# A third kept score tile in a two-sweep latent attention, with the shift additions on GpSimd

## The chip, the cores and the metric

The kernel runs on one core of one Trainium2 chip. A core has TensorE (PE, matrix products; PEld is its weight loading), VectorE (DVE), ScalarE (ACT), GpSimd (POOL) and SyncE (SP, which only issues DMAs here), and the memories SBUF and PSUM. The engines run on their own and wait for one another on semaphores. The metric is the device time of one execution in microseconds (us), as the median of several runs.

## The reference

The program is a chain of six layers on `x` (512 rows of 512) with a context `ctx_1024` of 8192 rows: a blockwise MLP over the context, a Mamba-like scan, a quantised feed-forward layer, the latent cross attention which the change touches, a channel attention, and a mixture of experts. The fourth one is:

```python
def _L1_xattn_ref(x, latents, Wq, Wkv, Wout, gm, bm, gl, bl):   # x: the context, latents: the normed rows
    scale = D_HEAD ** (-0.5)
    xn = layernorm(x, gm, bm)
    ln = layernorm(latents, gl, bl)
    q = ln @ Wq
    kv_input = jnp.concatenate([xn, ln], axis=-2)
    kv = kv_input @ Wkv
    k, v = jnp.split(kv, 2, axis=-1)
    q, k, v = (heads(q), heads(k), heads(v))
    q = q / scale
    sim = jnp.einsum('bhid,bhjd->bhij', q, k)
    sim = sim - jax.lax.stop_gradient(jnp.max(sim, axis=-1, keepdims=True))
    attn = jax.nn.softmax(sim, axis=-1)
    out = jnp.einsum('bhij,bhjd->bhid', attn, v)
    return out.transpose(0, 2, 1, 3).reshape(B, L, H * dh) @ Wout
```

There are 8 heads of 64, 512 queries and 8704 keys (8192 of the context and the 512 latents).

## The kernel before

The attention works in two sweeps over 17 chunks of 512 keys (`KCHUNKS`, `KEYS`). Heads are taken in four pairs (`PAIRS`), two heads side by side on the two halves of the partitions. All products are made in three parts out of a high and a low half of each float32 operand.

**First sweep** (`project_pe`, `project_act`, `project_dve`, 835 to 1320 us). PE projects the keys and values of chunk c, ACT evicts them, POOL makes the low halves of the context rows (`split_rest`, L1127), and SP stores keys and values to DRAM (`store_chunk`). Between the projections PE makes the scores of chunk c - 1, from which only the maximum per query is wanted. They come in halves of two head pairs, each with `BLOCK` = 8 tiles of 128 keys x 2 x 512 queries: tile i is key tile i // 2 of the half's pair i % 2. PE makes them in groups after unit 3, 9 and 15 of 16 (`GROUPS`: tiles 0 to 2, 3 to 5, 6 and 7) in three pairs of PSUM banks. A tile that only serves the maximum has one product of high halves (L2734); DVE takes the maximum straight from PSUM (L2048).

The last two tiles (i >= `COMPUTED` = 6) of 29 of the 34 halves are kept: `is_kept` leaves out the last halves. Such a tile gets all three products, ACT copies it to `kept_rows` with the key's scale (`keep_scores`, L1466), DVE takes the maximum from there (L2042), and SP stores both tiles to DRAM (`store_kept`, L831). A tile's bank pair is free for PE when DVE has taken the maximum (`s4_peak`) or, for a kept one, when ACT has copied it (`kept_out`). From chunk `LATE` = 12 on the groups lie closer (`groups_after`).

**Second sweep** (`attend_pe`, `exps`, `add_probs`, `load_turn`, 1320 to 1780 us). 34 blocks of one chunk and one half follow one another, first the near half of the heads (blocks 0 to 16), then the far one (17 to 33). 29 blocks use kept tiles (`kept_block`: 2 to 16 and 19 to 32). In such a block PE makes tiles 0 to 5 (`similarities`, L2829) with four products each, three for the score and one that adds the shift, minus the maximum, by a product of two rows. ACT takes the exponential from PSUM into `pT` (L1550), eight buffers. For tiles 6 and 7 SP loads the kept scores to `kept_back` (L889), double buffered by s, DVE adds the shift, which has been spread over the partitions once (`shift_wide`, L2101), and ACT takes the exponential from there (L1547). DVE adds every `pT` to `sums` (L2116), and PE multiplies the values by all eight in one run (`weigh_values`, L2853).

The order on each engine is that of the program text. The waits that matter: PE makes tile i of a block when the exponential that last used its banks is done (`s4_exp`). Exponential n waits until tile n - 8 has been multiplied and summed (`s4_pv`, `s4_sum`). On DVE the two shift additions of a block stand ahead of its eight sum additions. SP loads block j when the values of block j - 2 are multiplied (L883): keys, values, scale rows and then the kept scores. In the far half DVE also scales a part of the near result every second block (`near_scaled`). POOL has nothing to do in the second sweep until `near_lo` (L1148) near its end.

Of the kernel before, what the change touches and what calls it, by code (L numbers as in the profile page):

```python
# [11 lines left out]
P = 128  # L12
# [167 lines left out]
COMPUTED = 2 * (KT - 1)  # L180
# [103 lines left out]
def build(nc, a, out):  # L284
    ctx = ExitStack()
    with ctx:
# [29 lines left out]
        silu_warm = lasting("silu_warm", [P, 1])  # L316
        counts = lasting("counts", [P, 2, P], F32R)
# [137 lines left out]
        wout_lo = over("wout_lo", [P, DT, D], F32R)  # L455
        shift_cols = over("shift_cols", [P, PAIRS, TT, P], F32R)
        key_lo = s4("key_lo", [P, 2, PAIRS, KEYS], F32R)
# [15 lines left out]
        kept_rows = Map(nc, xn_at, xn_at + 8192)("kept_rows", [P, 2, 2, T])  # L473
        shift_near = Map(nc, xn_at, xn_at + 8192)("shift_near", [P, 2, 2, T])
# [3 lines left out]
        spread_ones = Map(nc, bc_at, bc_at + 2048)("spread_ones", [P, P], F32R)  # L478
# [91 lines left out]
        kept_dram = nc.dram_tensor("kept_rows_dram", [KCHUNKS, 2, P, 4 * T], F32, kind="Internal").ap()  # L570
# [148 lines left out]
        def near_scores(q):  # L719

            return q * 16 + 16

        def far_scores(q, s):
            return q * 16 + (LEFT * 16 + 16 + s * 16)
# [26 lines left out]
        def _(sp):  # L751
# [77 lines left out]
            def store_kept(c, half, rows):  # L829
                sp.wait_ge(*kept_out(kept_halves(c, half) * 2 + 2))  # L830
                sp.dma_start(rows[half], kept_rows[:].rearrange("p i e n -> p (i e n)")).then_inc(kept_stored.sem, 16)  # L831

            def project_turn(c, s, keys, rows, following=None, before=None):
# [5 lines left out]
                if before is not None:  # L839
                    store_kept(c - 1, 0, before)  # L840
                    if isinstance(c, int) and LATE <= c < LATE + 2:
                        store_kept(c - 1, 1, before)
# [4 lines left out]
                if before is not None and not (isinstance(c, int) and c >= LATE):  # L847
                    store_kept(c - 1, 1, before)
# [29 lines left out]
            sp.wait_ge(*kept_stored(16 * (2 * KCHUNKS - 5)))  # L878

            def load_turn(j, s, half, keys, rows, scales, scores=None):  # L880
                pairs = slice(2 * half, 2 * half + 2)
                scored = slice(0, KEYS if scores is None else KEYS - P)
                sp.wait_ge(*s4_pv((j - 1) * BLOCK))  # L883
                sp.dma_start(key_hi[:, s, pairs, scored].bitcast(F32), keys[0][:, pairs, scored]).then_inc(kv_loaded[s].sem, 16)
# [3 lines left out]
                if scores is not None:  # L888
                    sp.dma_start(kept_back[:, s].rearrange("p i e n -> p (i e n)"), scores[half]).then_inc(kept_loaded[s].sem, 16)  # L889
# [93 lines left out]
        def _(pool):  # L983
# [162 lines left out]

            pool.wait_ge(*o_hi(3))
# [46 lines left out]
        def _(act_e):  # L1194
# [264 lines left out]
            def keep_scores(c, half):  # L1459
                for i in range(COMPUTED, BLOCK):  # L1460
                    act_e.wait_ge(*peak_mm((c * 2 + half) * BLOCK + (i + 1)))
                    if i == COMPUTED and not (isinstance(c, int) and (c, half) == (0, 0)):
                        act_e.wait_ge(*kept_stored(kept_halves(c, half) * 16))
                    b = peak_place(c, half, i)
                    act_e.sem_inc(act_passed, 1)
                    nc.scalar.activation(kept_rows[:, i - COMPUTED], ps[:, b:b + 2], ACT.Copy,  # L1466
                                         scale=rs_all[:, bass.ds(c * KT + (KT - 1), 1)]).then_inc(kept_out.sem, 1)

            def project_act(c, s, turn, stores, follows):
                def keep(first, end):  # L1470
                    if isinstance(c, int) and c >= LATE:
                        for u in range(first, end):
                            for cp, half, tiles in groups_after(c, u):
                                if tiles[0] == COMPUTED and is_kept(cp, half):
                                    keep_scores(cp, half)
                    elif first % (4 * DT) == 4 * DT - 1:
                        keep_scores(c - 1, first // (4 * DT))
# [29 lines left out]
            def spread_back(p):  # L1507
                act_e.wait_ge(*spread_mm(p + 1))
                if p == 0:
                    act_e.wait_ge(*kept_stored(16 * (2 * KCHUNKS - 5)))  # L1510
                nc.scalar.activation(shift_wide(p), ps[:, 4:6], ACT.Copy).then_inc(spread_out.sem, 1)

            def exps(j, c, s, half):
# [5 lines left out]
                for i in range(BLOCK):  # L1519
# [18 lines left out]
                    if from_first:  # L1538
                        act_e.wait_ge(*kept_shifted(kept_before(j, half) * 2 + (i - COMPUTED + 1)))
# [6 lines left out]
                    if from_first:  # L1546
                        nc.scalar.activation(pT[:, i], kept_back[:, s, i - COMPUTED], ACT.Exp).then_inc(s4_exp.sem, 1)  # L1547
# [193 lines left out]
        def _(dve):  # L1741
# [292 lines left out]
            def peaks(c, half, tiles, first=False):  # L2034
                for i in tiles:
                    n = (c * 2 + half) * BLOCK + i
                    p, kt, b = half * 2 + i % 2, i // 2, peak_place(c, half, i)
                    if is_kept(c, half) and i >= COMPUTED:
                        dve.wait_ge(*kept_out(kept_halves(c, half) * 2 + (i - COMPUTED + 1)))
# [1177 lines left out]
```

## Time and profile before

| | |
|---|---|
| median of 3 runs | 2524.31 us (2522.81 to 2526.32) |
| profiled execution | 2520.99 us, span 2519.3 us |
| PE busy | 2415.6 us, 96% |
| DVE busy | 1860.6 us, 74% |
| ACT busy | 1186.5 us, 47% |
| POOL busy | 613.9 us, 24% |
| DMA, mean | 178 GB/s |

All times of the trace are from the span's start. Busy time of an engine is the union of its instructions; a busy PE need not be PE at its peak. A view of stretches gives the busy time of each engine in a window, the timeline gives instructions in order of time, with runs of equal ones merged (x8 with 9.17 us: eight instructions in 9.17 us), and a row on a source line gives least, median and longest duration.

### The profile page before, as it was taken

What the parts mean: (1) busy time and instruction counts of PE and PEld (TensorE: products, weight loads), DVE (VectorE), ACT (ScalarE), POOL (GpSimd) and SP (SyncE); (2) the same over time, 40 slices, a digit from 0 to 9 for tenths busy, and PEclk for the clock granted to TensorE, in tenths of its full rate; (3) what the DMA queues carried; (4) which work ended last, traced back from release to release, by engine and by line L of the source; (5) the groups of instructions that cost most, each with busy time, mean ns of one, the idle gap of its engine ahead of it and who ended that gap; (6) DMA issues with size and microseconds to landing.
All of it is one profiled execution on the core that took longest, in us unless ns stands there. A gap on an engine that the chain in (4) does not pass through costs nothing.

```text
span 2519.3 us, 32970 instructions
## 1 busy us (share of the span) xinstructions
PE 2415.6 (96%) x11317; PEld 1644.7 (65%) x11321; DVE 1860.6 (74%) x1935; ACT 1186.5 (47%) x1460; POOL 613.9 (24%) x419
## 2 busy tenths in 40 slices
PE   8999999998777999999999999999899999999998
PEld 6788877654334777777765445454687777777775
DVE  7888864499988577777787987999656756566664
ACT  2233332576355333333326666566444545555453
POOL 4655554498842211111110000000311000000000
PEclk9999999999978999999999999999999999999999
DMA  9667745721021455555525553455213666565663
GB/s 349 232 238 257 267 169 186 252 83 66 1 104 49 179 206 200 200 216 219 202 108 174 185 188 114 160 182 173 68 67 126 216 218 228 211 234 206 242 223 117
DMA packets 127265, 447.98 MB, mean 178 GB/s; under 512 B 11784, under 2 KB 42324, under 8 KB 92736
## 3 DMA queue, kind: packets, MB, share of 16 engines
q1 hardware_dynamic: 98608, 380.04, 42.2%
q10 hardware_dynamic: 28560, 66.66, 7.2%
q8 instruction: 59, 0.97, 0.2%
q14 instruction: 38, 0.31, 0.0%
HBM read 326.94 MB, written 119.71 MB: 177 GB/s over the span
## 4 chain that ended last, share of the span: by engine, by line
PE 85%; DVE 7%; POOL 2%; issue 2%; ACT 2%; DMA 1%; SPq 0%; DVEq 0%; ACTq 0%; POOLq 0%
PE ps L2422 20%; PE ps L2424 19%; PE ps L2423 19%; PE ps L2853 9%; PE ps L2829 8%; PE ps L2734 4%; DVE ps L1886 2%; POOL work L1075 1%; PE ps L3130 1%; PE ps L2546 1%; DVE work L1886 1%; POOL work L1056 1%; DMA wT_lo<-w_halves 0%; DVE ln_st L1746 0%; PE ps L3087 0%
## 5 line engine op out<-in xcount | busy, mean ns | idle before, releaser
L2116 DVE TENSOR_TENSOR sums<-sums,pT 128x1024 f32<-128x1024 f32 x272 | 314.9, 1224 | 54.0 <-ACT pT L1550 53.0
L2048 DVE SCALAR_TENSOR_TENSOR peak<-ps,rs_all,peak 128x1024 f32<-128x1024 f32 x214 | 263.7, 1277 | 47.8 <-PE ps L2734 47.3
L1550 ACT ACTIVATE pT<-ps,rs_all 128x1024 f32<-128x1024 f32 x214 | 220.1, 1123 | 163.3 <-PE ps L2829 163.3
L2853 PE MATMUL ps<-pT,values 128*64 128x512 f32 x1088 | 242.5, 596 | 0.0
L1127 POOL TENSOR_TENSOR cT_lo<-cT_raw,cT_hi 128x512 fp32r<-128x512 f32 x60 | 78.2, 1303 | 378.7 <-ACT cT_hi L1448 378.7
L2853 PEld LDWEIGHTS ps<-pT,values 128*64 128x64 f32 x1088 | 74.6, 137 | 146.2 <-issue 118.4
L2286 DVE TENSOR_TENSOR rgu_lo<-rgu_raw,rgu_hi 128x2048 fp32r<-128x2048 f32 x64 | 143.9, 2288 | 8.4 <-ACT rgu_hi L1639 8.4
L2546 PE MATMUL ps<-work,ident 128*128 128x512 f32 x256 | 126.7, 625 | 23.0 <-POOL work L1056 13.5
L1225 ACT ACTIVATE act<-ps 128x512 f32<-128x512 f32 x64 | 38.3, 599 | 222.2 <-PE ps L2424 221.1
L1018 POOL TENSOR_TENSOR ctx_lo<-ctx_raw,ctx_hi 128x512 fp32r<-128x512 f32 x64 | 106.5, 1664 | 105.7 <-DVE ctx_hi L1791 105.7
L2042 DVE TENSOR_TENSOR peak<-kept_rows,peak 128x1024 f32<-128x1024 f32 x58 | 68.5, 1221 | 77.1 <-ACT kept_rows L1466 77.1
L2280 DVE TENSOR_TENSOR sh_lo<-sh_raw,sh_hi 128x1536 fp32r<-128x1536 f32 x32 | 56.3, 1758 | 92.2 <-ACT sh_hi L1634 92.2
L1886 DVE TENSOR_TENSOR_SCAN ps<-ps,work 128x1024 f32<-128x1024 f32 x51 | 116.6, 2285 | 6.6 <-ACT ps L1367 6.6
L1439 ACT ACTIVATE values<-ps,rs_all 128x512 f32<-128x512 f32 x68 | 46.8, 688 | 158.3 <-PE ps L2424 158.1
L1639 ACT ACTIVATE rgu_hi<-rgu_raw 128x2048 fp32r<-128x2048 f32 x64 | 118.8, 1906 | 0.0
L1148 POOL TENSOR_TENSOR near_lo<-o_raw,near_hi 128x1024 fp32r<-128x1024 f32 x1 | 2.4, 2402 | 477.6 <-ACT near_hi L1529 477.6
L1367 ACT ACTIVATE ps<-delta,scan_small 128x512 f32<-128x512 f32 x128 | 82.9, 682 | 69.4 <-DVE work L1889 62.2
L1434 ACT ACTIVATE key_hi<-ps 128x512 fp32r<-128x512 f32 x68 | 40.7, 598 | 148.3 <-PE ps L2424 148.2
L1024 POOL TENSOR_TENSOR act_lo<-act,act_hi 128x512 fp32r<-128x512 f32 x64 | 95.2, 1487 | 50.3 <-DVE act_hi L1805 50.3
L2422 PE MATMUL ps<-xT_hi,ctxT_lo 128*128 128x512 f32 x256 | 102.2, 399 | 0.9 <-DVE xT_lo L1776 0.9
L2422 PE MATMUL ps<-ctx_hi,act_lo 128*128 128x512 f32 x256 | 101.7, 397 | 0.3
L2546 PEld LDWEIGHTS ps<-work,ident 128*128 128x128 f32 x256 | 49.1, 198 | 81.0 <-issue 39.2
(502 smaller groups left out, 6692.1 us busy)
## 6 DMA issues: line engine op xcount, KB each, us to landing
rgu_raw<-in_r_gate_up SPq DMA_DIRECT2D x64, 1024.0 KB, 4.8
rd_raw<-in_r_down SPq DMA_DIRECT2D x32, 1024.0 KB, 4.9
kept_rows_dram<-kept_rows SPq DMA_DIRECT2D x29, 1024.0 KB, 3.9
kept_back<-kept_rows_dram SPq DMA_DIRECT2D x29, 1024.0 KB, 6.8
sh_raw<-in_s_parts SPq DMA_DIRECT2D x32, 768.0 KB, 4.3
key_rows<-key_hi SPq DMA_DIRECT2D x17, 1024.0 KB, 3.9
key_rows<-key_lo SPq DMA_DIRECT2D x17, 1024.0 KB, 5.9
value_rows<-values SPq DMA_DIRECT2D x17, 1024.0 KB, 7.9
```

The lines of the kernel that those rows point to most:

```text
L1550: nc.scalar.activation(pT[:, i], ps[:, b:b + 2], ACT.Exp, scale=rs_all[:, bass.ds(c * KT + attend_tile(j, i)[1], 1)]).then_inc(s4_exp.sem, 1)
L1639: nc.scalar.activation(rgu_hi[:, j % 2, i], rgu_raw[:, j % 2, i], ACT.Copy).then_inc(rgu_high.sem, 1)
L1886: nc.vector.tensor_tensor_scan(drive if far(n) else state, state, drive, 0.0, ALU.mult, ALU.add).then_inc(sc_scan, 1)
L2048: nc.vector.scalar_tensor_tensor(peak[:, p], ps[:, b:b + 2], rs_all[:, bass.ds(c * KT + kt, 1)], peak[:, p], ALU.mult, ALU.max).then_inc(s ...
L2116: nc.vector.tensor_tensor(sums[:, p], sums[:, p], pT[:, i], ALU.add).then_inc(s4_sum.sem, 1)
L2286: nc.vector.tensor_tensor(rgu_lo[:, j % 2, i], rgu_raw[:, j % 2, i], rgu_hi[:, j % 2, i].bitcast(F32), ALU.subtract).then_inc(rgu_low.sem, 1)
L2422: nc.tensor.matmul(o, l_lo, r_hi, start=start, stop=False)
L2423: nc.tensor.matmul(o, l_hi, r_lo, start=False, stop=False)
L2424: return nc.tensor.matmul(o, l_hi, r_hi, start=False, stop=stop)
L2546: done = nc.tensor.matmul(ps[:, 0], ident[:], work[:, n % RING, e], start=g == 0 and e == 0, stop=g == SGS - 1 and e == SG - 1)
L2829: done = nc.tensor.matmul(ps[:, b + e], key[rows], query[rows], start=m == 0, stop=m == len(parts) - 1)
L2853: done = nc.tensor.matmul(ps[e * DK:(e + 1) * DK, 6 + p], values[:, s, kt, h * DK:(h + 1) * DK], pT[:, i, e], start=start and kt == 0, sto ...
```

## The change

Three tiles of each kept half are kept instead of two: `COMPUTED` goes from 6 to 5, `KEPT` is 3. Tile 5 gets three products in the first sweep, ACT copies it ahead of `values_out` of its unit (after unit 11), separately from tiles 6 and 7. It has a place of its own in SBUF, `kept_first`; SP stores a half in two DMAs, and both kept halves ahead of the chunk's stores. In the second sweep PE leaves out tile 5, SP loads the kept scores in two DMAs (`back_first` and `kept_back`) ahead of the keys, and the shift additions, now three per block, go from DVE to POOL, in a loop of its own (`shift_kept`) which waits only for the loads and for the spread shift. The amounts in DRAM grow from 1 to 1.5 MB per half.

```diff
-COMPUTED = 2 * (KT - 1)
+COMPUTED = 2 * KT - 3
+KEPT = BLOCK - COMPUTED
...
+        back_first = Map(nc, back_at, back_at + 8192)("back_first", [P, 2, 2, T])
...
+        kept_first = Map(nc, counts_at, counts_at + 4096)("kept_first", [P, 2, T])
...
+        def kept_tile(i):
+            return kept_rows[:, i - COMPUTED - 1] if i > COMPUTED else kept_first[:]
+
+        def back_tile(s, i):
+            return kept_back[:, s, i - COMPUTED - 1] if i > COMPUTED else back_first[:, s]
...
             def store_kept(c, half, rows):
-                sp.wait_ge(*kept_out(kept_halves(c, half) * 2 + 2))
-                sp.dma_start(rows[half], kept_rows[:].rearrange("p i e n -> p (i e n)")).then_inc(kept_stored.sem, 16)
+                sp.wait_ge(*kept_out(kept_halves(c, half) * KEPT + 1))
+                sp.dma_start(rows[half][:, 0:2 * T], kept_first[:].rearrange("p e n -> p (e n)")).then_inc(kept_stored.sem, 16)
+                sp.sem_inc(sp_passed, 1)
+                sp.wait_ge(*kept_out(kept_halves(c, half) * KEPT + KEPT))
+                sp.dma_start(rows[half][:, 2 * T:KEPT * 2 * T], kept_rows[:].rearrange("p i e n -> p (i e n)")).then_inc(kept_stored.sem, 16)
...
                     store_kept(c - 1, 0, before)
-                    if isinstance(c, int) and LATE <= c < LATE + 2:
+                    if not (isinstance(c, int) and c >= LATE + 2):
                         store_kept(c - 1, 1, before)
...
                 store_chunk(c, s, keys, rows)
-                if before is not None and not (isinstance(c, int) and c >= LATE):
-                    store_kept(c - 1, 1, before)
...
                 sp.wait_ge(*s4_pv((j - 1) * BLOCK))
+                if scores is not None:
+                    if isinstance(j, int) or half == 0:
+                        sp.sem_inc(sp_passed, 1)
+                        sp.wait_ge(*shift_T(PAIRS))
+                    sp.dma_start(back_first[:, s].rearrange("p e n -> p (e n)"), scores[half][:, 0:2 * T]).then_inc(kept_loaded[s].sem, 16)
+                    sp.dma_start(kept_back[:, s].rearrange("p i e n -> p (i e n)"), scores[half][:, 2 * T:KEPT * 2 * T]).then_inc(kept_loaded[s].sem, 16)
                 sp.dma_start(key_hi[:, s, pairs, scored].bitcast(F32), keys[0][:, pairs, scored]).then_inc(kv_loaded[s].sem, 16)
...
                 load_scales(scales, s)
-                if scores is not None:
-                    sp.dma_start(kept_back[:, s].rearrange("p i e n -> p (i e n)"), scores[half]).then_inc(kept_loaded[s].sem, 16)
...
+            def shift_kept(half, s, turn):
+                pool.wait_ge(*kept_loaded[s](turn))
+                for i in range(COMPUTED, BLOCK):
+                    nc.gpsimd.tensor_tensor(back_tile(s, i), back_tile(s, i), shift_wide(2 * half + i % 2), ALU.add).then_inc(kept_shifted.sem, 1)
+
+            pool.wait_ge(*spread_out(PAIRS))
+            with pool.Fori(0, LEFT) as q:
+                shift_kept(0, 1, near_scores(q))
+                shift_kept(0, 0, near_scores(q))
+            shift_kept(0, 1, near_scores(LEFT))
+            with pool.Fori(0, LEFT) as q:
+                shift_kept(1, 0, far_scores(q, 0))
+                shift_kept(1, 1, far_scores(q, 1))
...
-            def add_probs(j, half, s=0, turn=0):
-                if kept_block(j):
-                    dve.wait_ge(*kept_loaded[s](turn))
-                    if isinstance(j, int) and j == 2:
-                        dve.wait_ge(*spread_out(PAIRS))
-                    for i in range(2):
-                        nc.vector.tensor_tensor(kept_back[:, s, i], kept_back[:, s, i], shift_wide(2 * half + i), ALU.add).then_inc(kept_shifted.sem, 1)
+            def add_probs(j, half):
...
-                        if i < 2 and (is_kept(c, 0) if half else is_kept(c - 1, 1)):
-                            pe.wait_ge(*kept_out(kept_halves(c, half) * 2 - (1 - i)))
+                        if i < 3 and (is_kept(c, 0) if half else is_kept(c - 1, 1)):
+                            pe.wait_ge(*kept_out(kept_halves(c, half) * KEPT - (1, 0, 2)[i]))
```

## Rows read from the trace of the kernel before

**Rows 1.** The page's chain of work that ended last, by engine.

```profile
PE 85%; DVE 7%; POOL 2%; issue 2%; ACT 2%; DMA 1%; SPq 0%; DVEq 0%; ACTq 0%; POOLq 0%
```

**Rows 2.** Busy time by stretch: length, each engine with instructions, PE clock, DMA.

```profile
core 0: us, PE busy (x) PEld busy (x) DVE busy (x) ACT busy (x) POOL busy (x), PEclk, DMA share, GB/s
835.00:1320.00 485.00, 483.81 (x2325) 345.67 (x2326) 370.80 (x344) 176.31 (x249) 84.00 (x65) 1.00 0.50 196
1358.00:1552.00 194.00, 193.35 (x1196) 96.02 (x1196) 171.58 (x151) 119.08 (x120) 0.00 (x0) 1.00 0.53 172
1582.00:1763.00 181.00, 181.00 (x1124) 90.79 (x1124) 166.75 (x152) 112.99 (x113) 0.00 (x0) 1.00 0.55 179
```

**Rows 3.** Timeline of ACT, second sweep: start, length, instruction, count, [idle before].

```profile
1356.58 6.16 ACT L1550 ACTIVATE pT<-ps,rs_all 128x1024 f32<-128x1024 f32 x6
...
1371.71 6.14 ACT L1550 ACTIVATE pT<-ps,rs_all 128x1024 f32<-128x1024 f32 x6 [7.10 <-PE ps L2829]
...
1526.52 6.13 ACT L1550 ACTIVATE pT<-ps,rs_all 128x1024 f32<-128x1024 f32 x6 [4.87 <-PE ps L2829]
...
1596.60 6.14 ACT L1550 ACTIVATE pT<-ps,rs_all 128x1024 f32<-128x1024 f32 x6 [4.89 <-PE ps L2829]
...
1751.51 6.14 ACT L1550 ACTIVATE pT<-ps,rs_all 128x1024 f32<-128x1024 f32 x6 [4.88 <-PE ps L2829]
```

**Rows 4.** Timeline of PE in block 9: first products of two score tiles.

```profile
1451.39 0.44 PE L2829 MATMUL ps<-q_lo,key_hi 64*128 64x512 f32 x2
...
1452.36 0.48 PE L2829 MATMUL ps<-q_lo,key_hi 64*128 64x512 f32 x2
```

**Rows 5.** Timeline of DVE over the same block.

```profile
1450.40 9.17 DVE L2116 TENSOR_TENSOR sums<-sums,pT 128x1024 f32<-128x1024 f32 x8 [1.46 <-ACT pT L1550]
...
1459.49 2.35 DVE L2101 TENSOR_TENSOR kept_back<-kept_back,shift_near 128x1024 f32<-128x1024 f32 x2
```

**Rows 6.** Timeline of PE in the first sweep: two products of a kept tile.

```profile
1010.34 0.40 PE L2734 MATMUL ps<-q_hi,key_hi 64*128 64x512 f32 x2
1010.57 0.40 PE L2734 MATMUL ps<-q_hi,key_lo 64*128 64x512 f32 x2
```

**Rows 7.** ACT's copies (least, median, longest ns), and the page's landing of kept stores.

```profile
L1466 ACT ACTIVATE kept_rows<-ps,rs_all x58: 1107/1114/1118, 846.8 to 1254.8; 128x1024 f32<-128x1024 f32 x58
...
kept_rows_dram<-kept_rows SPq DMA_DIRECT2D x29, 1024.0 KB, 3.9
```

**Rows 8.** POOL's near_lo in the timeline; DVE's sum additions that start in 1766 to 1769.

```profile
1768.00 2.40 POOL L1148 TENSOR_TENSOR near_lo<-o_raw,near_hi 128x1024 fp32r<-128x1024 f32 x1 [477.57 <-ACT near_hi L1529]
...
L2116 DVE TENSOR_TENSOR sums<-sums,pT x2: 1224/1910/2596, 1766.9 to 1768.9; 128x1024 f32<-128x1024 f32 x2
```

**Rows 9.** Groups by line and shape: count, busy us, mean ns, idle before.

```profile
L1075 POOL TENSOR_TENSOR work<-x_conv,bc_first 128x1024 f32<-128x1024 f32 x32 | 75.1, 2381 | 37.2 <-DMA bc_first<-bc_rows 37.2
...
L1150 POOL TENSOR_TENSOR w_lo<-w_first,w_hi 128x2048 fp32r<-128x2048 f32 x1 | 4.6, 4593 | 9.2 <-ACT w_hi L1575 9.2
...
L2286 DVE TENSOR_TENSOR rgu_lo<-rgu_raw,rgu_hi 128x2048 fp32r<-128x2048 f32 x64 | 143.9, 2288 | 8.4 <-ACT rgu_hi L1639 8.4
```

**Rows 10.** Timelines of DVE and POOL in the first stage, around 111 and 114 us.

```profile
110.76 0.68 DVE L1795 TENSOR_TENSOR ctxT_lo<-ctxT_raw,ctxT_hi 128x512 fp32r<-128x512 f32 x1
...
113.61 1.83 DVE L1815 TENSOR_TENSOR unit_lo<-unit_raw,unit_hi 128x512 fp32r<-128x512 f32 x1
...
110.92 1.67 POOL L1018 TENSOR_TENSOR ctx_lo<-ctx_raw,ctx_hi 128x512 fp32r<-128x512 f32 x1 [1.56 <-DVE ctx_hi L1791]
113.59 1.30 POOL L1024 TENSOR_TENSOR act_lo<-act,act_hi 128x512 fp32r<-128x512 f32 x1 [1.00 <-DVE act_hi L1805]
```

**Rows 11.** Timeline of the first sweep: DVE with a PSUM input beside POOL.

```profile
1000.91 1.30 POOL L1127 TENSOR_TENSOR cT_lo<-cT_raw,cT_hi 128x512 fp32r<-128x512 f32 x1 [5.95 <-ACT cT_hi L1448]
...
1001.55 0.68 DVE L2013 TENSOR_TENSOR key_lo<-ps,key_hi 128x512 fp32r<-128x512 f32 x1
```

**Rows 12.** DMA queues from 1360 to 1540 us: packets, MB, share of 16 engines.

```profile
q1 hardware_dynamic: 17204, 33.22, 56.9%
```

**Rows 13.** Busy time in a stretch ahead of the attention; columns as in rows 2.

```profile
710.00:835.00 125.00, 97.64 (x382) 61.34 (x386) 94.86 (x142) 70.51 (x101) 50.08 (x36) 0.79 0.11 38
```

## What the change should do to the time

> **What bounds the kernel now.** I read the page first: the chain of work that ended last is 85% TensorE (PE), with VectorE (DVE) at 7% [rows 1]. A share over the whole kernel says nothing about the two stages that the change touches, so I cut the span by stage next. In the first sweep (835 to 1320 us) PE works 483.8 of 485 us, DVE 370.8, GpSimd (POOL) 84. In the kept blocks of the second sweep PE works 193.4 of 194 (near half) and 181.0 of 181 (far half), DVE 171.6 and 166.8, that is 88% and 92%, and POOL nothing [rows 2]. So both sweeps are bound by PE, and in the second DVE follows closely.
>
> The period of a kept block is read from ScalarE's (ACT's) exponentials, one group of six for each block: from 1371.71 to 1526.52 us lie 12 blocks, 12.90 us each, and from 1596.60 to 1751.51 lie 12 more, 12.91 each [rows 3]. The fifth and the sixth score tile of a block start at 1451.39 and 1452.36, so a tile costs PE 0.97 us [rows 4]. DVE's eight additions to the sums take 9.17 us back to back (1.146 each; one timed alone is 1.22 [rows 8]), and its two shift additions 2.35 [rows 5].
>
> **First sweep: what is added.** There are 29 kept halves. In each the sixth tile (number 5) gets three products in place of one. The six products of a kept pair follow one another every 0.23 us (1010.34, 1010.57) [rows 6]. That is 2 x 0.23 x 29 = 13.3 us, on PE, on the path. ACT gets 29 copies of 1.11 us [rows 7]; it works 176 of 485 us in this stage [rows 2] and idles the rest, so they are hidden; if that cover were gone they would cost 32 us. DVE trades a maximum out of PSUM for one out of SBUF, which must wait for ACT's copy, as its neighbours do now. Queued behind that wait on DVE are the last two maxima, which come after a PE group that is still ahead at that moment. On SP the stores of a kept half now come ahead of the chunk's stores, and wait for ACT twice; behind them stand the chunk's three stores and the next chunk's load, which move back by about 2 us. The kept stores land 3.9 us after issue [rows 7], and the next copy into the same rows comes some 10 us later (the half's period of 15 us less the 5 us by which tile 5 is earlier). I take 0 for all of this and 5 us as the upper bound.
>
> **Second sweep: what is removed.** 29 tiles of 0.97 us leave PE: a block would need 12.90 - 0.97 = 11.93 us, and DVE without its shift additions 9.2. If nothing else set the pace, this gives back 29 x 0.97 = 28.1 us, and 14.8 net.
>
> **Second sweep: what is moved to GpSimd.** Three additions per block, each 128x1024 in float32 with both inputs in SBUF. The same operation and shape takes 2.38 us on POOL in the scan [rows 9]: 7.1 us of an engine that is idle, and started a block ahead. Taken alone this would be free. The rows that decide are those where such an operation meets a DVE one that reads two SBUF inputs:
> - POOL computed near_lo from 1768.00 to 1770.40. A sum addition was issued on DVE at 1768.89. It took 2596 ns, where its twin took 1224 [rows 8], and so ended at 1771.49, 1.09 after POOL. It did not run slower, it stood still until POOL was done.
> - In the first stage POOL ran act_lo from 113.59 for 1.30 us; DVE's unit_lo, issued at 113.61, took 1.83 us and ended 0.55 after POOL. A subtraction of the same shape that DVE issued ahead of POOL, at 110.76, took 0.68 [rows 10].
> - The other way round: DVE's ctxT_lo ran 110.76 to 111.44, POOL's ctx_lo was issued at 110.92, took 1.67 in place of 1.30 and ended 1.15 after DVE [rows 10].
> - Where DVE reads one input from PSUM nothing happens: key_lo at 1001.55 took 0.68 with POOL at work since 1000.91 [rows 11].
>
> So the sum additions (sums and pT, both in SBUF) and the shift additions (both in SBUF) exclude each other, as if there were one way into SBUF for a second input of DVE and for POOL, which I call the port. Whoever waits has its start-up hidden: DVE then needs 1.09, and POOL 0.15 less than alone (1.15 against 1.30), 2.23. A block has three alternations and five free additions: 3 x (1.09 + 2.23) + 5 x 1.146 = 15.7 us. That is above PE's 11.93 and above today's 12.90. The additions move from an engine that had room to a place where they cost 2.23 us in place of 1.15 each and hold up the same engine. The Trainium skill, "SBUF — State Buffer", section "Who interferes with whom", has this as a rule: a DVE instruction with two SBUF inputs contends with a GpSimd instruction that reads SBUF, and the second to issue blocks fully. By it the sum is the one above; if the two merely shared bandwidth, or not even that, it would be the first rival. The trace agrees (2596 ns against 1224).
>
> What waits then: exponential n needs the sum of n - 8, so with DVE late ACT stalls on its eight buffers, the scores stay in PSUM, and PE waits for ACT. The DMAs grow by 0.5 MB per block on 2.3; their queue is busy 56.9% of a 12.9 us block, 7.3 us, so about 8.9 of 15.7 afterwards [rows 12]: hidden, though the keys now land after the scores.
>
> **The sum.** Near half: the additions of blocks 2 to 16 fall in blocks 2 to 15, since a block's scores are loaded one block ahead, and block 2 holds two sets. 14 x 2.82 + one more set of 6.7 = 46.2; block 2 took 15.1 us (1356.58 to 1371.71) instead of 12.9, which absorbs 2.2; block 16 has none and wins 0.97: +43.0. Far half: 13 x 2.82 = 36.7, plus 0.9 in the block before it, which hosts the first set (eight computed tiles on PE, 12.90 + 2 x 0.97 = 14.8, to 15.7), less 0.97 in the last: +36.6. DVE has some further work in the far half (92% of 12.9 us against 88%, 0.5 us per block [rows 2]), in which POOL may use the port; I take 0, and 8 us at most. Together 13.3 + 43.0 + 36.6 = +92.9 us. The profiled execution took 2520.99 us (span 2519.3), the median 2524.31, 3.3 more; on the median this gives 2617.2.
> Bounds of the period: if the port is held only for the streaming part, it is the difference between widths: DVE 2288 - 1224 = 1.06, POOL 4593 - 2400 = 2.19 [rows 8, 9]: 8 x 1.06 + 3 x 2.19 = 15.1, 0.6 x 27 = 16 us less in all, 2601. If nothing is hidden, 8 x 1.22 + 3 x 2.38 = 16.9, 1.2 x 27 = 32 more; with the 8 and the 5 from above 2662.
>
> **Rivals.**
> - The additions hide, as on an idle engine: 2524.3 - 14.8 = 2509.5. For it: POOL does nothing there, and DVE falls to 9.2 of 11.9. Against it: [rows 8, 10]. It decides if at least 3.3 of the 6.7 us per block overlap, that is if the period falls below 12.90 - 13.3/29 = 12.44. Chance 0.07, and 0.03 for an overlap of about that size, with the time unchanged.
> - DVE, with a full queue, keeps the port, and POOL gets it only when DVE has run dry. The three exponentials then wait for POOL: 9.2 + 3 x 2.38 + an exponential of 1.1 = 17.4 us, 1.7 more in 27 blocks, 2663; with a wait between them some 2680. Nothing in the trace shows who is served when both queue. Chance 0.06.
> - PE's clock. It is granted in full through both sweeps; in the stretch 710 to 835, where PE sits idle more, it is 0.79 [rows 13]. At 0.79 PE's 11.93 become 15.1, still below 15.7. It decides below 0.76; at 0.65 a block takes 18.4, 2.6 more, 2690. The gaps would be short and in every block. Chance 0.04.
> - Forecast as above: 0.80.
>
> **The numbers.** 2617 is the likeliest. The range 2592 to 2664 takes in both bounds and half of the second rival. A measurement of this kernel can tell about 0.2% (5 us) from no change. Slower 0.90 (forecast, second and third rival), unchanged 0.03, faster 0.07.
>
> **What would show it.** DVE's sum additions in the second sweep have a median or mean well above 1.22 us, some at 3.3 (1.09 behind a POOL operation of 2.23), and POOL's additions last 2.4 to 3.5. The group of ACT's exponentials comes every 15.7 us. PE waits for ACT there, and ACT for DVE's sums. The first sweep is longer by 13 us. A period of 11.9 with sum additions at 1.22 would prove me wrong; so would a period of 15.7 with undisturbed DVE durations, where another wait would be the cause.

## The result, and the profile after

The changed kernel takes 2613.7 us (median of 5 runs, 2607.74 to 2614.7) against 2524.3 before (5 runs, 2517.14 to 2526.32): a ratio of 1.036, 95% interval 1.035 to 1.038. It is slower by 89 us, as forecast (2617). Its profiled execution took 2607.74 us (span 2605.9), 86.6 us of span more than before. The table shows where they lie, from the start of one stage or block to the next. A block's start is its first exponential; the first sweep ends with PE's first score product of the second one, 1.3 us ahead of that in both:

| stretch | before, us | after, us | difference | forecast |
|---|---|---|---|---|
| ahead of the first sweep | 835.1 | 835.2 | 0 | 0 |
| first sweep | 484.4 | 500.4 | +16.1 | +13.3 |
| blocks 0 and 1 | 35.8 | 35.5 | -0.3 | 0 |
| near half, blocks 2 to 16 | 195.3 | 231.0 | +35.7 | +43.0 |
| blocks 17 and 18 | 31.8 | 33.0 | +1.2 | +0.9 (in the far half's sum) |
| far half, blocks 19 to 32 | 180.5 | 214.4 | +33.9 | +35.7 |
| block 33 and the rest | 755.1 | 755.2 | 0 | 0 |
| together | 2519.3 | 2605.9 | +86.6 | +92.9 |

The page's lines on the two new or changed operations. The columns are busy us, mean ns of one, and idle time before with what ended it.

```profile
L2142 DVE TENSOR_TENSOR sums<-sums,pT 128x1024 f32<-128x1024 f32 x272 | 486.7, 1856 | 21.9 <-ACT pT L1582 16.2
...
L1167 POOL TENSOR_TENSOR back_first<-back_first,shift_near 128x1024 f32<-128x1024 f32 x15 | 68.4, 4559 | 119.2 <-ACT shift_far L1543 66.2
```

A sum addition took 1224 ns alone [rows 8]; now the mean is 1856. The chain of work that ended last has changed with it. The page's shares can't be held against [rows 1], since the chain of the changed kernel reaches back only to 1262 us and covers about half of the span. So here are the chains of the kept blocks alone, before (1357 to 1764 us) and after (1373 to 1850):

```profile
by line: PE ps L2853 52.2%; PE ps L2829 44.7%; DMA scale_rows<-sd_rows_dram 1.2%; ACT pT L1550 0.6%; PE ps L2891 0.4%; issue 0.3%; SPq L886 0.2%; ACT o_raw L1536 0.1%; SPq L884 0.1%; SPq L865 0.1%; SPq L885 0.1%; ACTq L1544 0.0%; ACTq L1545
```

```profile
by line: issue 43.1%; POOL kept_back L1167 25.5%; POOL back_first L1167 11.3%; PE ps L2879 6.3%; PE ps L2855 4.8%; DMA kept_back<-kept_rows_dram 2.4%; DVE sums L2142 2.3%; DMA scale_rows<-sd_rows_dram 1.5%; ACT pT L1579 0.9%; ACT pT L1582 0
```

PE was 97% of it and is 11%; POOL, which did nothing there, is 37%. "issue" is time for which the profile shows no releaser, so the chain says that PE no longer sets the pace, and not yet what does. The same views as [rows 2], of the first sweep and of the near and far blocks:

```profile
core 0: us, PE busy (x) PEld busy (x) DVE busy (x) ACT busy (x) POOL busy (x), PEclk, DMA share, GB/s
835.00:1336.20 501.20, 498.66 (x2443) 356.76 (x2444) 373.71 (x344) 205.83 (x278) 83.98 (x65) 1.00 0.56 220
1390.00:1603.00 213.00, 184.66 (x1012) 86.49 (x1010) 205.36 (x111) 116.19 (x112) 149.92 (x41) 0.91 0.51 173
1636.00:1850.00 214.00, 183.04 (x1006) 83.30 (x1004) 213.00 (x126) 116.68 (x113) 130.01 (x39) 0.93 0.53 183
```

In the first sweep PE still works all the time. In the second the bound has moved: PE idles 28 and 31 us, DVE is busy 205.36 of 213 us and 213 of 214. DVE is idle for 7.6 and 1.0 us in all, and whatever else is slow there (a landing DMA, PE's clock) can hardly cost more than that. But DVE has less to do than before, since the shift additions have left it: a busy DVE here is largely a DVE that stands still inside an instruction. The timeline shows it, around 1409 us:

```profile
1408.19 11.11 DVE L2142 TENSOR_TENSOR sums<-sums,pT 128x1024 f32<-128x1024 f32 x4
1408.86 2.77 POOL L1167 TENSOR_TENSOR back_first<-back_first,shift_near 128x1024 f32<-128x1024 f32 x1 [5.09 <-DMA kept_back<-kept_rows_dram]
1411.58 6.63 POOL L1167 TENSOR_TENSOR kept_back<-kept_back,shift_near 128x1024 f32<-128x1024 f32 x2
```

Four sum additions take 11.11 us: one of 1.15 that ran before POOL got in, and three of 3.32, each with a POOL addition inside. That is the alternation of 1.09 and 2.23 that was forecast, 3.32. Who waits for whom from 1380 to 1850 us (us in total, times, longest):

```profile
POOL back_first L1167 <- DMA kept_back<-kept_rows_dram: 164.3, 23, 33.6
...
ACT pT L1582 <- DVE sums L2142: 62.8, 22, 6.8
ACT pT L1579 <- DVE sums L2142: 41.4, 21, 2.3
PE ps L2879 <- ACT pT L1579: 47.2, 28, 3.6
```

ACT waits for DVE's sums and PE for ACT: the eight buffers are full. POOL waits only for its data, which says that its engine has time; what it takes away is DVE's.

### The profile page after: what moved, and what is told of

Its sections match the earlier page's. It is cut to its first block, busy times and chain, and to the rows that moved or that the text cites. A ratio compares the mean times of both kernels' runs of the same rounds, so it can differ in the third digit from the quotient of the medians.

```text
span 2605.9 us, 33155 instructions
## 1 busy us (share of the span) xinstructions
PE 2435.4 (93%) x11205; PEld 1643.9 (63%) x11205; DVE 1971.3 (76%) x1877; ACT 1224.5 (47%) x1489; POOL 921.0 (35%) x506
## 4 chain that ended last, share of the span: by engine, by line
PE 32%; issue 8%; POOL 7%; DVE 2%; DMA 1%; ACT 1%; SPq 0%; DVEq 0%; POOLq 0%; ACTq 0%
PE ps L2448 9%; PE ps L2450 8%; PE ps L2449 8%; POOL kept_back L1167 5%; POOL back_first L1167 2%; PE ps L2879 2%; PE ps L2855 2%; PE ps L3156 1%; DVE sums L2142 1%; PE ps L2760 1%; DMA kept_back<-kept_rows_dram 0%; PE ps L3113 0%; DVE peak L2080 0%; PE ps L3182 0%; DMA sh_raw<-in_s_parts 0%
## 5 line engine op out<-in xcount | busy, mean ns | idle before, releaser
L2142 DVE TENSOR_TENSOR sums<-sums,pT 128x1024 f32<-128x1024 f32 x272 | 486.7, 1856 | 21.9 <-ACT pT L1582 16.2
L2879 PE MATMUL ps<-pT,values 128*64 128x512 f32 x1088 | 264.2, 627 | 54.5 <-ACT pT L1579 47.2
L1582 ACT ACTIVATE pT<-ps,rs_all 128x1024 f32<-128x1024 f32 x185 | 195.0, 1119 | 155.2 <-PE ps L2855 91.3
L2080 DVE SCALAR_TENSOR_TENSOR peak<-ps,rs_all,peak 128x1024 f32<-128x1024 f32 x185 | 229.0, 1277 | 50.4 <-PE ps L2760 49.9
L2572 PE MATMUL ps<-work,ident 128*128 128x512 f32 x256 | 126.3, 623 | 23.8 <-POOL work L1073 12.9
L1167 POOL TENSOR_TENSOR back_first<-back_first,shift_near 128x1024 f32<-128x1024 f32 x15 | 68.4, 4559 | 119.2 <-ACT shift_far L1543 66.2
L2448 PE MATMUL ps<-rgu_hi,xg_lo 128*80 128x512 f32 x256 | 101.9, 398 | 0.0
```

The lines of the kernel that those rows point to most:

```text
L1167: nc.gpsimd.tensor_tensor(back_tile(s, i), back_tile(s, i), shift_wide(2 * half + i % 2), ALU.add).then_inc(kept_shifted.sem, 1)
L1582: nc.scalar.activation(pT[:, i], ps[:, b:b + 2], ACT.Exp, scale=rs_all[:, bass.ds(c * KT + attend_tile(j, i)[1], 1)]).then_inc(s4_exp.sem, 1)
L2080: nc.vector.scalar_tensor_tensor(peak[:, p], ps[:, b:b + 2], rs_all[:, bass.ds(c * KT + kt, 1)], peak[:, p], ALU.mult, ALU.max).then_inc(s ...
L2142: nc.vector.tensor_tensor(sums[:, p], sums[:, p], pT[:, i], ALU.add).then_inc(s4_sum.sem, 1)
L2448: nc.tensor.matmul(o, l_lo, r_hi, start=start, stop=False)
L2572: done = nc.tensor.matmul(ps[:, 0], ident[:], work[:, n % RING, e], start=g == 0 and e == 0, stop=g == SGS - 1 and e == SG - 1)
```

## The experiments

Each ratio is taken against runs of the kernel before from the same session (medians 2520.5 to 2521.5). Periods are from one exponential group to the next, as in [rows 3].

### e1: the same three kept tiles, their shifts on DVE

```diff
-            def shift_kept(half, s, turn):
...
-            def add_probs(j, half):
+            def add_probs(j, half, s=0, turn=0):
+                if kept_block(j):
+                    dve.wait_ge(*kept_loaded[s](turn))
...
+                    for i in range(COMPUTED, BLOCK):
+                        nc.vector.tensor_tensor(back_tile(s, i), back_tile(s, i), shift_wide(2 * half + i % 2), ALU.add).then_inc(kept_shifted.sem, 1)
```

> The changed kernel, with its three shift additions per block back on DVE, ahead of the sums, and POOL without any. Exclusion theory: DVE needs 11 x 1.146 = 12.6 us per kept block and some 0.5 more in the far half, PE 11.9, so blocks of about 12.7 and 13.2 us; the first sweep keeps its 16 us: 2524 + 16 - 3 + 4 = 2541 us, sum additions all at 1.22. Rival, that the third tile, its DMAs or its waits cost the time wherever the addition runs: about 2614.

Measured 2531.3 us, ratio 1.0032 (1.0021 to 1.0043). The page's line of the sums, and busy time by stretch in the near and the far half:

```profile
L2135 DVE TENSOR_TENSOR sums<-sums,pT 128x1024 f32<-128x1024 f32 x272 | 315.4, 1224 | 17.8 <-ACT pT L1569 16.3
```

```profile
1420.00:1560.00 140.00, 139.46 (x851) 68.24 (x849) 140.00 (x124) 93.22 (x93) 0.00 (x0) 1.00 0.67 228
1640.00:1780.00 140.00, 135.05 (x794) 61.68 (x792) 139.31 (x128) 91.95 (x91) 1.47 (x1) 1.00 0.62 214
```

The additions are back at 1224 ns and some 80 of the 89 us are gone, by nothing but the engine that adds. Kept tiles, loads and first sweep are those of the changed kernel, so they are not the loss. DVE now has eleven operations of about 1.15 us, 12.6 us a block, and is busy all the time, yet the near blocks come every 11.9 us, which is PE's pace. I expected 12.6. The reason is the buffers: ACT may be eight tiles ahead of the sums, so a DVE that is 0.7 us late per block costs nothing until the lead is used up. In the far half it is: from block 25 on the periods are 12.2 to 13.8, and the block behind the near half pays 1.6 us back (18.5 for 16.9).

### e2: one of the three shift additions on GpSimd, two on DVE

```diff
-                for i in range(COMPUTED, BLOCK):
-                    nc.gpsimd.tensor_tensor(...).then_inc(kept_shifted.sem, 1)
+                for i in (COMPUTED,):
+                    nc.gpsimd.tensor_tensor(...).then_inc(pool_shifted.sem, 1)
...
+                    for i in range(COMPUTED + 1, BLOCK):
+                        nc.vector.tensor_tensor(...).then_inc(kept_shifted.sem, 1)
```

> The changed kernel with one shift addition per block (tile 5) on POOL and two on DVE. Exclusion theory: 3.3 + 9 x 1.146 = 13.6 us per block, some 13.8 in the far half, 28 x 0.8 = 22 us over the kernel before plus 16 in the first sweep: 2562 us. If POOL ran independently, DVE would need 11.5 and PE 11.9: 2524 + 16 - 28 = 2512.

Measured 2556.1 us, ratio 1.0136 (1.0117 to 1.0156), 25 us more than e1. The number is near what the theory said, but only part of the mechanism is: the sum additions have a mean of 1296 ns, 20 us too much in all 272, and DVE idles 20 us in the near half. What happens instead stands in the timelines from 1447 to 1475 us, first GpSimd, then DVE, then ACT:

```profile
1450.16 16.94 POOL L1168 TENSOR_TENSOR back_first<-back_first,shift_near 128x1024 f32<-128x1024 f32 x1 [9.04 <-DMA kept_back<-kept_rows_dram]
...
1447.80 9.16 DVE L2150 TENSOR_TENSOR sums<-sums,pT 128x1024 f32<-128x1024 f32 x8
1456.88 2.35 DVE L2135 TENSOR_TENSOR kept_back<-kept_back,shift_near 128x1024 f32<-128x1024 f32 x2
1459.16 5.75 DVE L2150 TENSOR_TENSOR sums<-sums,pT 128x1024 f32<-128x1024 f32 x5
1468.56 1.94 DVE L2150 TENSOR_TENSOR sums<-sums,pT 128x1024 f32<-128x1024 f32 x1 [3.65 <-ACT pT L1581]
...
1467.39 1.06 ACT L1581 ACTIVATE pT<-back_first 128x1024 f32<-128x1024 f32 x1 [5.44 <-POOL back_first L1168]
```

GpSimd's addition is issued at 1450.16 and ends at 1467.10. DVE runs thirteen additions meanwhile at their undisturbed 1.15 us and falls dry at 1464.91; GpSimd ends 2.2 us later, the time that it needs by itself. So it got in only when DVE had stopped, and DVE had stopped because ACT was waiting for that very addition. This is the rival "DVE keeps the port", which had a chance of 0.06. It does not happen each time: of the 29 additions eleven take 7.5 to 16.9 us, and the others pass at the next hand-over or run free (2.3 to 3.4). In the far half the long ones end without a gap on DVE. One was issued at 1654.93 and took 13.11 us, to 1668.04; DVE's timeline there:

```profile
1663.46 2.34 DVE L2150 TENSOR_TENSOR sums<-sums,pT 128x1024 f32<-128x1024 f32 x2
1665.73 0.94 DVE L2164 RECIPROCAL o_raw<-o_raw  x1
1666.81 1.38 DVE L2166 TENSOR_TENSOR o_raw<-o_raw  x1
```

GpSimd got in with the reciprocal, which reads one SBUF input (1665.73 and 2.3 us are 1668.04), and the small product behind it, 0.29 us in the kernel before, stood still until then. All the long ones, six in the far half and five in the near one, end 2.2 to 2.4 us after such a reciprocal or the beginning of a gap.

### e3: two kept tiles as before, their shifts on GpSimd

```diff
-                    for i in range(2):
-                        nc.vector.tensor_tensor(kept_back[:, s, i], ...)
...
+                for i in range(2):
+                    nc.gpsimd.tensor_tensor(kept_back[:, s, i], ...)
```

> The kernel before, with two kept tiles, and only its two shift additions moved to POOL. Exclusion theory: 2 x 3.3 + 6 x 1.146 = 13.5 us per block against 12.9, 28 x 0.6 = 17 us: 2541. If POOL ran independently, PE stays the bound at 12.9: 2524.

Measured 2538.8 us, ratio 1.0061 (1.0044 to 1.0079): the move alone, without a third tile, costs 15 to 17 us. The sums have a mean of 1614 ns, 106 us too much, 1.83 for each of the 58 GpSimd additions. Most of it is absorbed: DVE then needs about 12.8 us of PE's 12.90, and most blocks keep 12.9. The loss sits in a few blocks: in the longest, 20.3 us, a GpSimd addition ends that took 17.9 us. So the time came out near the 2541 expected, but not by a period of 13.5 in every block.

### e4: the additions of the changed kernel at half their width

```diff
-  nc.gpsimd.tensor_tensor(back_tile(s, i), back_tile(s, i), shift_wide(2 * half + i % 2), ALU.add)
+  nc.gpsimd.tensor_tensor(back_tile(s, i)[:, :, 0:T // 2], back_tile(s, i)[:, :, 0:T // 2], shift_wide(2 * half + i % 2)[:, :, 0:T // 2], ALU.add)
...
-  nc.scalar.activation(pT[:, i], back_tile(s, i), ACT.Exp)
+  nc.scalar.activation(pT[:, i], back_tile(s, i), ACT.Exp, scale=0.0)
```

> The changed kernel, in which POOL adds the shift to the first 256 of 512 queries of each kept tile only, and the exponential of kept tiles is taken with scale 0, so the rest of the shift and the kept tiles' weights are left out; every instruction on the other engines is as before in size. Exclusion for the length of an operation: 3 x (1.09 + 1.15) + 5 x 1.146 = 12.45 us per block, 2524 + 16 - 13 = 2527. If each POOL operation cost a fixed stall whatever its length: as the changed kernel, 2614.

Measured 2518.9 us, ratio 0.9990 (0.9981 to 1.0000). The same count of operations, waits and DMAs, half the elements, and over 90 us are gone. From 1360 to 1800 us, by line and shape:

```profile
L2142 DVE TENSOR_TENSOR sums<-sums,pT 128x1024 f32<-128x1024 f32 x263 | 389.1, 1550 | 16.5 <-ACT pT L1582 15.6
...
L1167 POOL TENSOR_TENSOR kept_back<-kept_back,shift_near 128x512 f32<-128x512 f32 x30 | 66.2, 2226 | 0.0
```

DVE's 389.1 us are 87.7 more than 263 x 1.146, 1.01 us for each of the 87 GpSimd additions. Per block 8 x 1.146 + 3 x 1.01 = 12.2, and the blocks come every 12.0 to 12.1. So the price is the time of GpSimd's streaming, not one of a wait or a semaphore.

### e5: no shift addition to speak of

As e4, with 8 columns of each head in place of 256 (`0:8`).

> The changed kernel with the shift additions cut to 8 of 512 queries and the exponential of kept tiles taken with scale 0, so the shift of the kept tiles and their weights are left out. Everything else of the change stays: three kept tiles, the DMAs, the waits on POOL. Exclusion theory: PE sets the pace at 11.93 us per block, 2524 + 16 - 27 = 2513. If the stores, loads and waits of the third tile had a price of their own in the second sweep, the blocks stay above 12.5 us and the time above 2530.

Measured 2517.2 us, ratio 0.9991 (0.998 to 1.0001). Near and far blocks come every 11.98 and 11.90 us: 12.90 - 0.97 = 11.93 was forecast for PE alone. The gain on PE is real, 0.9 to 1.0 us a block. The near half is shorter by 9.2 us and the far half by 14.1, and the first sweep takes 16.1 of these 23.4 back. Blocks without a shift to speak of also show that the third tile's loads and waits set no period of their own.

### e6: GpSimd writes, and reads nothing

```diff
-  nc.gpsimd.tensor_tensor(back_tile(s, i), back_tile(s, i), shift_wide(2 * half + i % 2), ALU.add)
+  nc.gpsimd.memset(back_tile(s, i)[:, :, first:T], 0.0)
```

with one 8-column addition ahead of the three, and the exponential with scale 0.

> The kernel of the run before it, with each kept tile also overwritten by a memset on POOL (0.95 us each, three per block), which writes SBUF and reads nothing; the scores of the kept tiles are left out. If only two readers exclude each other: no DVE sum addition above 1.3 us, and 2513. If any POOL instruction that touches SBUF excludes DVE: sum additions of 1.9 to 2.0 us beside the memsets, three in each block.

Measured 2517.9 us, ratio 0.9991 (0.9976 to 1.0005), e5's time. Timelines around 1457 us:

```profile
1459.41 0.94 POOL L1169 MEMSET back_first<- 128x1008 f32 x1
1460.29 1.84 POOL L1169 MEMSET kept_back<- 128x1024 f32 x2
...
1454.76 9.20 DVE L2144 TENSOR_TENSOR sums<-sums,pT 128x1024 f32<-128x1024 f32 x8 [2.71 <-ACT pT L1584]
```

Three writes of 128x1024 (the first 16 columns short) pass beside eight additions, and neither is lengthened (9.20 us for eight, 9.17 in [rows 5]). Of all 272 sum additions one is above 1.3 us, at 2.59, and it is so in e5 too, without memsets. A GpSimd operation that only writes does not stop DVE; e4 and this one together put the cost on its reads. The Trainium skill says the same in "SBUF — State Buffer", section "Who interferes with whom": a DVE instruction with two SBUF inputs contends with a GpSimd one that reads, "not with one that only writes it".

### e7: the first sweep's extra products alone

```diff
-                    if is_kept(c, half) and i >= COMPUTED:
+                    if is_kept(c, half) and i >= COMPUTED - 1:
```

in the kernel before, in PE's score products: tile 5 gets three products and is used as before, for its maximum.

> The kernel before, with three products in place of one for tile 5 in the first sweep and nothing else: no copy by ACT, no store. The prediction's term of 29 x 0.46 = 13.3 us: 2537.6. If the 16.0 us by which the first sweep of the changed kernel is longer are all products, 2540; if the copy and stores add the difference, the first sweep is longer by 13.3 here.

Measured 2536.7 us, ratio 1.0071 (1.0054 to 1.0088). The first sweep takes 498.3 us, 13.9 more (13.3 forecast), and the rest is that of before. The changed kernel has 16.1 there. The other 2.1 belong to what I had put at 0: copies, stores and the maximum that waits for a copy. 1.3 of them are idle time of PE (2.5 us in the changed kernel, 1.2 here), all of it after 1253 us, and the waits from 1253 to 1336 us in the changed kernel name one piece:

```profile
ACT kept_first L1496 <- DMA kept_rows_dram<-kept_rows: 6.1, 1, 6.1
```

### e8: e5 with the kept scores loaded behind the keys

```diff
                 sp.wait_ge(*s4_pv((j - 1) * BLOCK))
+                sp.dma_start(key_hi[:, s, pairs, scored].bitcast(F32), ...)
...
+                load_scales(scales, s)
                 if scores is not None:
...
-                sp.dma_start(key_hi[:, s, pairs, scored].bitcast(F32), ...)
```

> The kernel of e5 (three tiles kept, no shift addition at all, so its result is not the reference's softmax) with one thing put back: SP loads a block's kept scores after its keys, values and scale rows, as in the kernel before. In e5 block 2 took 18.7 us against 15.1 before, 3.6 more, while all later blocks took 11.98. Theory, keys late: block 3's keys land later because 1.5 MB of scores stand ahead of them in the queue; block 2 falls to about 15.1 and the near half (block 2 to 17) from 186.1 to about 182.5, the whole to 2513.5 us (ratio about 0.9975). Rival, the order of the loads is hidden and block 2 is long for another reason (its own first loads): block 2 stays at 18.4 to 18.7, the near half at 186, the whole at 2517 (0.999).

Measured 2510.8 us, ratio 0.9951 (0.9936 to 0.9967). Block 2 takes 13.7 us against e5's 18.7, and the near half 179.9 against 186.1. What PE waited for at the start of block 3, first in e5, then here:

```profile
PE ps L2855 <- DMA scale_rows<-sd_rows_dram: 4.3, 1, 4.3
```

```profile
PE ps L2855 <- DMA scale_rows<-sd_rows_dram: 0.2, 1, 0.2
```

So the order of the loads was not hidden: with 1.5 MB of scores ahead of them, the keys of block 3, the first that is loaded while its predecessor already runs, come 4.3 us late. PE then also pays in clock: behind this wait the granted clock of e5 is at the lower of its two levels for 3.4 us from 1389.7, and in e8 it does not fall there. I expected 15.1 for block 2 as before and it is 13.7; PE has a tile less to make, which is 0.97 of the 1.4.

### e9: the third tile in the near half only, shifts on DVE, keys first

```diff
-def attend_groups(j):
+def attend_groups(j, half):
...
+def computed(half):
+    return COMPUTED + half
...
-                    for i in range(COMPUTED, BLOCK):
+                    for i in range(computed(half), BLOCK):
```

> A version put together from what the runs before showed, complete in what it computes: all shift additions on DVE (as e1), the third tile kept only in the near half of the heads, scores loaded after the keys. Sum from measured terms: first sweep, 15 halves with 0.5 us each (e7: 13.9 us for 29) and their copies and stores about 1, +8; near half, e1's period of 12.06 against 12.90 and block 2 back at its 15.1: 187.3 - 3.4 = 184 against 195.3, -11; far half as before, 0 (with three there e1 won 5.4 us of 180.5 and paid 1.7 behind the last near block). Together -3, a ratio of 0.9988: at the edge of what can be told. Rival, block 2 stays at 18.4 for another reason than the order of the loads: near half 187.3, together 0, a ratio of 1.000. Rival, the far half's gain was worth more than its first-sweep price: then e9 is no better than e1 (1.0032).

Measured 2521.6 us, ratio 0.9997 (0.9988 to 1.0006). First sweep +8.5, near half -9.6, blocks 17 and 18 +1.6, far half -0.2: nothing is left. The near half gave less than expected because DVE, with 12.6 us of work per block, used up its lead after five blocks here (periods 11.9, then 12.5 from block 8) and paid 1.6 us behind it. A third kept tile costs 0.5 us in the first sweep and wins 0.97 on PE at best; with the DVE work of its shift neither e1 nor e9 shows a net gain.

e8 and e9 are read for their times alone. Their output is not what it should be (e8's is not e5's, e9's is not the reference's), and no run here shows why. So the word "complete" in e9's expectation does not hold, and neither is a version to use. If keys were read too early there, part of e8's gain would not be real. What speaks against it is that PE's first product of block 3 starts at 1389.56 us, 6.9 us after the keys were issued, and that both e8 and the kernel before wait there for the same DMA.

## Why the prediction was right, and where its terms were off

**The mechanism.** It said that sum additions and shift additions exclude each other and that this, not PE, sets the period. e1 (same work on DVE, some 80 us less), e4 (half the width, half the price) and e6 (writes only, no price) show each part: the engine, the streaming, the read. The first rival, that the additions hide, is out by the 1856 ns. That the number came so close is partly luck: on the profiled executions it is 86.6 us for 92.9, with a near half that is 7.3 too low, a first sweep that is 2.8 too high and a far period that is right by two errors. Two slips in the sum hardly count: 15.69 less 12.90 is 2.79 and not 2.82, and a second set is 3 x 2.17 = 6.5 and not 6.7, together 1 us.

**The price of one GpSimd addition.** Forecast: 3.32 less the 1.146 that a sum addition takes anyway, 2.17. Measured from 1360 to 1860 us, by line and shape:

```profile
L2142 DVE TENSOR_TENSOR sums<-sums,pT 128x1024 f32<-128x1024 f32 x256 | 467.1, 1895 | 17.4 <-ACT pT L1582 12.8 <-ACT pT L1579 4.4
...
L1167 POOL TENSOR_TENSOR kept_back<-kept_back,shift_near 128x1024 f32<-128x1024 f32 x30 | 98.0, 3288 | 0.0
```

467.1 - 256 x 1.146 = 173.7 us for 87 additions, 2.00 each: some of them ran in part while DVE was dry, or held up the small product behind the far half's reciprocal (1.38 us in place of 0.29) and not a sum. That makes 8 x 1.146 + 3 x 2.00 = 15.2 us a block in place of 15.7. The near blocks 3 to 15 have a mean of 15.3.

**Near half, +35.7 for +43.0.** This term was mis-sized in two places. The 13 blocks 3 to 15 at 15.3 instead of 15.7 are 5 us. Block 2, with its two sets, was to take 12.90 + 2.82 + 6.7 = 22.4 us and takes 18.4; block 16, which was to win 0.97, takes 13.9 instead of 11.7 and gives 2 us of it back. Block 2's second set was a term without a price there: e5 has no shift to speak of and takes 18.7 us in this block, e1 with its shifts on DVE 18.8, so its length is set by the keys that land late (below), and GpSimd's additions add nothing to it. The blocks are not regular, as I had pictured them. Blocks 3 to 15 take 11.8 to 22.1 us, since GpSimd adds its three in one go when a block's scores have landed, and the next block or two run free. Part of such a batch is taken up by the eight buffers, which the sum had not reckoned with and which e1 shows.

**Far half and the block before it, +35.1 for +36.6.** From block 20 to 31 the period is 15.7 as forecast, but by two errors that cancel: 2.00 in place of 2.17, and 0.5 us of further DVE work per block (0.5 from the 92% and 88% of [rows 2]) that I had set to 0 with a bound of 8. With both, 15.2 + 0.5 = 15.7. The sum over the half is a little less, since block 19, the first of them, ran in 11.9 us (I put this down to the lead of the buffers, which no run singles out), while block 32 took 14.2.

**First sweep, +16.1 for +13.3.** The products cost 13.9 (e7), 0.48 per tile instead of 0.46. The step that failed is the one that put copies and stores at 0: they cost 2.1, within the bound of 5. ACT's copy of a later half waited 6.1 us for the store ahead of it; "the next copy comes some 10 us later" left out that near the sweep's end the groups lie closer and stores queue behind one another.

**The loads.** "Hidden, though the keys now land after the scores" was wrong for block 3. In e5 that is 4.3 us of PE's wait, and block 2 takes 18.7 us where 15.1 were needed before, with no shift addition to speak of. The changed kernel's 18.4 are no more than that, and with the keys first (e8) the block takes 13.7.

**GpSimd kept out.** The second rival was given 0.06 and happens in 3 of the 29 batches of the changed kernel (18.4, 9.7 and 13.1 us), and in 11 of 29 in e2. In the changed kernel's timeline:

```profile
1456.97 18.44 POOL L1167 TENSOR_TENSOR back_first<-back_first,shift_near 128x1024 f32<-128x1024 f32 x1 [7.55 <-DMA kept_back<-kept_rows_dram]
1475.38 5.63 POOL L1167 TENSOR_TENSOR kept_back<-kept_back,shift_near 128x1024 f32<-128x1024 f32 x2
```

The near additions into `back_first` have a mean of 4559 ns for two such among fifteen. With all three on GpSimd it costs little: DVE falls dry for 3.7 us and 0.6 us before these two get in, and ran at its own pace until then. With one of three (e2) it is most of the loss: there four gaps of 3.6 to 3.7 us in the near half are 15 of the 20 us in which DVE idles. The step that failed here is the judgement of the chance, 0.06: the traces of before had only isolated DVE instructions beside GpSimd's, and none of a full queue.

**PE's clock.** The third rival did not decide. The granted clock is 0.91 and 0.93 in the two stretches above, 1.00 before: it falls twelve times to the lower of its two levels (1.2 GHz of 2.4), for 3.4 to 10.2 us each, 72 us in all, in the stage where PE now waits for ACT again and again. As DVE was busy nearly all the while, the falls found cover; no run singles out what they cost.

## What to carry to other kernels

An engine that looks idle is not free: before moving elementwise work to GpSimd, check whether its instruction reads SBUF while DVE runs additions with two SBUF inputs, and count GpSimd's streaming time as DVE time. Here an addition of 1.15 us on DVE became 2.00 us of a standing DVE. And weigh what the saved work can give at best (28 us on PE) against its price elsewhere (16 us in the first sweep) before the transport is designed.

## What the runs showed that I had not expected

- Who gets in when both engines queue is not settled by who asked first. GpSimd's addition passed at the next hand-over in most cases, and took up to 18.4 us behind a gapless stream of DVE additions in others (1456.97 us above; 16.94 us in e2), until DVE fell dry or came to an instruction with one SBUF input. Where within DVE's current addition the request came does not tell them apart: 0.55 us into it, one had passed after 2.90 us (e2) and one took 13.1 (changed kernel). What decides which of the two happens stays open. The Trainium skill, "SBUF — State Buffer", section "Who interferes with whom", has issue order decide who blocks; the second to issue does block here, but behind up to fourteen instructions and not behind one.
- Once GpSimd has got in and its next additions are queued behind, the two alternate strictly, every 3.32 us.
- A store that lands late can cost PE's clock. The first sweep with the third tile stored took 500.4 to 500.5 us in the profiled executions of the changed kernel, e2, e4, e5 and e6, but 502.3 in those of e1 and e8, with the same code there. In these two ACT's copy of one kept tile waited 7.4 to 7.5 us for the store ahead of it and not 6.1, PE then waited 1.4 to 1.5 us for the values that ACT evicts behind that copy, and the granted clock fell to the lower of its two levels (1.2 GHz of 2.4) for 3.4 us. In all others it was 1.00 throughout. From e8, the two waits, and the stretch with the columns of [rows 2]:

```profile
ACT kept_first L1496 <- DMA kept_rows_dram<-kept_rows: 7.4, 1, 7.4
PE ps L2448 <- ACT values L1469: 1.4, 1, 1.4
```

```profile
1262.80:1266.20 3.40, 3.40 (x10) 2.27 (x11) 3.40 (x5) 0.87 (x2) 1.59 (x1) 0.50 0.75 308
```
